# A two-layer cross-attention and FFN kernel on one core: keys and values split into high and low parts in the first stage, the routing step folded into the last stage, and three smaller reorderings

## What is computed

```python
x = x + L0_xattn(layernorm(x), ctx)     # 16 heads, scores through a latent of 32 numbers per context row
x = x + L0_ffn(layernorm(x))            # one 512x512 product, int4 weights dequantised, bias
x = x + L1_xattn(layernorm(x), ctx)     # 16 query heads of 96, 4 K/V heads; keys and values from
                                        # concat([ctx, layernorm(x)]): 1601 + 256 rows; then Wo
x = x + L1_ffn(layernorm(x))            # H + delta, below

# L1_ffn: H = x W^T + b ; z = x A (rank 32)
# logits = 0.5 * H_slice / max|H_slice| + 0.5 * delta_slice / max|delta_slice|   (maxima over ALL batches)
# probs = softmax(logits) ; soft top-2 weights w ; delta = ((z * (w @ LiMEs)) @ Bmat) * 0.5
```

## Time and profile before

| | |
|---|---|
| median of 3 runs | 2047.75 us (2040.28 to 2049.16) |
| profiled execution: time, span | 2043.46 us, 2041.7 us |
| mean granted TensorE clock | 0.950 |
| busy: PE, DVE, ACT, POOL | 94%, 55%, 46%, 32% |
| stage 1, to its last PE work | 0 to about 304 us |
| stage 2 | 309 to 1021 us |
| stage 3 | 1024 to 2006 us |
| stage 4 | 2009 to 2042 us |

### The profile page before, as it was taken

How to read it: one execution, slowest core, us unless ns; L and a number is a source line. 1 busy time by engine, 2 the same in 40 slices (tenths; PEclk the granted TensorE clock), 3 DMA queues, 4 the chain that set the end, 5 groups by cost and what they waited for, 6 DMA issues and landing times. The chain is left out here.

```text
span 2041.7 us, 23682 instructions
## 1 busy us (share of the span) xinstructions
PE 1922.5 (94%) x8690; PEld 1368.1 (67%) x8690; DVE 1118.8 (55%) x2093; ACT 944.3 (46%) x1826; POOL 653.1 (32%) x504
## 2 busy tenths in 40 slices
PE   6999998999999999998869999999999999999986
PEld 6999984444555556464637777767777777777752
DVE  1433325666666665652266666666666566664433
ACT  1332322444344334343127666655666466665640
POOL 0000000000000000000028777756776577765740
PEclk9999995999899999999769999999999999999996
DMA  5556733000111010010261232213222222212112
GB/s 176 157 170 204 226 121 70 1 11 17 50 34 42 31 42 27 11 52 26 80 167 45 75 85 75 60 30 86 74 72 75 76 79 62 56 49 57 31 31 97
DMA packets 109697, 149.51 MB, mean 73 GB/s; under 512 B 28777, under 2 KB 87529, under 8 KB 106510
## 3 DMA queue, kind: packets, MB, share of 16 engines
q1 hardware_dynamic: 101630, 145.36, 24.9%
q10 hardware_dynamic: 7952, 2.64, 0.6%
HBM read 96.52 MB, written 51.39 MB: 72 GB/s over the span
## 5 line engine op out<-in xcount | busy, mean ns | idle before, releaser
L1366 POOL TENSOR_TENSOR pl<-pf,ph 128x512 fp32r<-128x512 f32 (+1 forms) x480 | 640.9, 1352 | 300.9 <-ACT pf L1533 299.2
L1530 ACT ACTIVATE ph<-ps 128x512 fp32r<-128x512 f32 (+1 forms) x480 | 288.5, 601 | 352.8 <-PE ps L1437 351.8
L1605 DVE TENSOR_REDUCE pm<-ps 128x1 f32<-128x464 f32 (+1 forms) x512 | 317.9, 635 | 119.9 <-PE ps L1383 113.5
L1132 DVE TENSOR_REDUCE pm<-ps 128x1 f32<-128x400 f32 (+1 forms) x512 | 264.2, 567 | 103.1 <-PE ps L970 100.2
L1031 ACT ACTIVATE pr<-ps 128x512 f32<-128x512 f32 (+1 forms) x416 | 219.4, 602 | 194.3 <-PE ps L909 193.0
L1533 ACT ACTIVATE pf<-ps 128x512 f32<-128x512 f32 (+1 forms) x480 | 289.2, 603 | 0.2 <-POOL pl L1366 0.2
L1355 POOL MEMSET vf<- 128x96 f32 x1 | 0.2, 178 | 711.2 <-POOLq L685 711.2
L1383 PE MATMUL ps<-kh,qh 96*128 96x464 f32 (+1 forms) x512 | 199.6, 399 | 21.9 <-DMA ql<-q_scr 12.9
L922 PE MATMUL ps<-pr,cv 128*64 128x512 f32 (+1 forms) x832 | 208.1, 616 | 0.0
L1435 PE MATMUL ps<-qh,kh 104*128 104x512 f32 (+1 forms) x480 | 194.7, 406 | 1.4 <-issue 1.4
L1452 PE MATMUL ps<-ph,vh 128*97 128x512 f32 (+1 forms) x480 | 194.3, 405 | 0.0
(11 more groups left out here) (222 smaller groups left out, 2648.8 us busy)
## 6 DMA issues: line engine op xcount, KB each, us to landing
woT<-wo_turned SPq DMA_DIRECT2D x16, 1536.0 KB, 9.2
cnat<-in_ctx_dram SPq DMA_DIRECT2D x16, 768.0 KB
q_scr<-qst SPq DMA_DIRECT2D x48, 256.0 KB, 2.4
kf<-k_scr SPq DMA_DIRECT2D x16, 696.4 KB, 4.8
vf<-v_scr SPq DMA_DIRECT2D x16, 672.0 KB
v_scr<-vst SPq DMA_DIRECT2D x64, 144.0 KB, 2.3
k_scr<-kst SPq DMA_DIRECT2D x36, 192.0 KB, 4.7
wo_turned<-wo_out SPq DMA_DIRECT2D x32, 192.0 KB, 2.8
```

The lines of the kernel that those rows point to most:

```text
L1132: dve.reduce_max(pm[:, j, ch:ch + 1], src[:, 0:cuts[ch][1]], AX).then_inc(done["dve"], 1)
L1366: pool.tensor_tensor(pl[0:m, n % 2, cols], pf[0:m, half, :], ph[0:m, n % 2, cols].bitcast(F32), ALU.subtract).then_inc(plo, 1)
L1530: act.activation(ph[0:keys[kt], n % 2, cols], src, ACT.Exp, scale=S1).then_inc(phi, 1)
L1605: ins = dve.reduce_max(pm[:, j, ch:ch + 1], at[:, 0:cuts[ch][1]], AX)
```

## The change

Five things are changed together.

* **Split in the first stage.** Keys and values are split into high and low parts while they are in PSUM in `context_products` (ACT high, DVE low, for every group), `k_scr` and `v_scr` hold both parts, and `grouped_attention` loads them straight into `kh`, `kl`, `vh`, `vl`. `kst` has one buffer for each j and `vst` one in all. The values lie in `v_scr` by row, so that one head's load takes runs of 96 numbers (384 B).
* **First step of the third stage prepared in the second.** Three SBUF tensors `home` outlive the stages; the keys and queries of step 0 are loaded into them by `load_first_group`, and step 0's maxima run beside step 15 of stage 2 (`maxima` with `s <= S`). Units 5 to 9 of batch 2 move from steps 14 and 15 into `after()`.
* **Routing in the third stage.** `mixture` is gone: x, z and the small tiles stay in SBUF, and the H product of the last batch is issued between routing steps.
* **Norms.** `layernorm` calls back for one item at seven points rather than for two at three.
* **Small loads** are issued by SP ahead of the key stores of pieces 1 to 4. The norm of batch 0 moves from piece 2 to piece 6.

```diff
-def layernorm(dve, chain, out, x, st, mv, v, t, u, y, pause=lambda: None):
+def layernorm(dve, chain, out, x, st, mv, v, t, u, y, pause=lambda: None, between=lambda: None):
+    between()
     chain.link(dve.bn_stats(st[:, 0, :], x[:, 0, :]))
+    between()
     chain.mark(dve.bn_stats(st[:, 1, :], x[:, 1, :]))
...
     for i in range(TT):
+        between()
         last = dve.tensor_scalar(out[:, i, :], x[:, i, :], mv[:, i, 0:1], y[:, i:i + 1], ALU.subtract, ALU.mult)
```

First stage, ACT and DVE (the SP side stores both parts: keys by j as before, values in one DMA for three tiles rather than four):

```diff
+            def values_hi(n, t):
+                m = rows_in(n, t)
+                act.wait_ge(*turned(("v", n, t)))
+                if t == 0 and n:
+                    act.wait_ge(v_st, v_stored(n - 1))
+                act.copy(vst[0:m, 0, t, :], bank_of(("v", n, t))[0:m, HD0:WV]).then_inc(v_hi, 1)
...
+            def keys_lo(n, j):
+                k = SIZES[n % NP]
+                dve.wait_ge(k_hi, n * KB + j + 1)
+                dve.tensor_tensor(kst[j][:, 1, 0:k], bank_of(("k", n, j))[:, 0:k], kst[j][:, 0, 0:k], ALU.subtract)\
+                    .then_inc(done["dve"], 1)
...
-                if n == 0:
-                    load_small()
...
                 if n + 2 < N:
                     load(n + 2)
+                load_small(n)
```

Second stage:

```diff
         def maxima(s, first, end):
-            return [("max", s, i) for i in range(first, end)] if s < S else []
+            return [("max", s, i) for i in range(first, end)] if s <= S else []
...
         def after():
             e = B - 1
-            return [("raise", S - 1), ("xt", e, 0, 0), ("xt", e, 0, 1), ("ffn", e, 0), ("ffn", e, 1),
+            return [("raise", S - 1), ("q", e - 1, 5), ("q", e - 1, 6), ("xt", e, 0, 0), ("xt", e, 0, 1),
+                    ("ffn", e, 0), ("ffn", e, 1), ("q", e - 1, 7), ("q", e - 1, 8), ("q", e - 1, 9),
                     ("xt", e, 1, 0), ("xt", e, 1, 1)] + [("q", e, u) for u in range(NU)]
...
+                    act.copy(qst[:, u % 2, 0, 0:width(u)].bitcast(F32R), src[:, 0:width(u)]).then_inc(qhi, 1)
```

Third stage (`FIRST = 4`):

```diff
             if s == 0:
-                return maxima
+                return [None] * 12 + maxima
...
+            load_v(0, 0, FIRST, v0_in)
+            load_values(0)
+            load_k(1, 0)
+            load_q(1, 0)
             load_wo(0)
             load_x(0)
...
             for s in range(S):
...
+                sp.wait_ge(s_mm, (s + 1) * KT * 2)
                 if s + 3 < S:
+                    load_k(s + 3, 0)
+                    load_q(s + 3, 0)
+                if s + 2 < S:
+                    load_k(s + 2, 1)
+                    load_q(s + 2, 1)
+                    sp.wait_ge(av_mm, (s + 1) * KT)
+                    load_values(s + 2)
...
+            pe.wait_ge(to_pe, 2)
+            pe.matmul(bank(3)[:, 0:2], ones2[:, :], dg[:, :], start=True, stop=True).then_inc(from_pe, 1)
+            for t in range(TT):
+                for c in range(DC):
+                    pe.matmul(bank(t), xT[:, c, t * P:(t + 1) * P], w1T[:, c, :], start=(c == 0), stop=False)
+            pe.wait_ge(to_pe, 3)
```

More of the change, by code:

```diff
@@ L1458, in values @@
                 mm.then_inc(av_mm, 1)
-            pe.wait_ge(const, 5)
-            for item in beside(-1):
-                ring_item(*item)
-            max_rows(0)
-            pe.wait_ge(w_small, 48)
             for s in range(S):
+                if s == 1:
+                    pe.wait_ge(w_small, 48)
                 items = iter(beside(s))
@@ L1489, in _ @@
                 ring_item(*item)
+            pe.wait_ge(exp_done, 2 * S * KT)
+            pe.wait_ge(o_done, 2 * S)
+            pe.wait_ge(mix_ones, 2)
+            pe.wait_ge(to_pe, 1)
+            pe.matmul(bank(2)[0:2, 0:P], pmx[:, :], ident[:, :], start=True, stop=True).then_inc(from_pe, 1)
+            pe.wait_ge(to_pe, 2)
[4 more added lines that the diff above has]
+            pe.wait_ge(to_pe, 3)
+            for b in range(B):
+                mm = pe.matmul(bank(2)[0:NE, b * P:(b + 1) * P], wt[:, b, :], ident[:, :], start=True, stop=True)
+            mm.then_inc(from_pe, 1)
+            pe.wait_ge(to_pe, 4)
+            pe.wait_ge(w_mix, 48)
+            pe.matmul(bank(3)[0:R, :], li[:, :], wT[:, :], start=True, stop=True).then_inc(from_pe, 1)
+            pe.wait_ge(bm_done, 1)
+            for n in range(B * TT):
+                b, t = divmod(n, TT)
+                if t == 0:
+                    pe.wait_ge(zp_done, b + 1)
+                if 4 <= n < (B - 1) * TT:
+                    pe.wait_ge(y_done, n - 3)
+                pe.matmul(delta_bank(n), zp[:, b, t * P:(t + 1) * P], bm[:, :], start=(b < B - 1), stop=True)\
+                    .then_inc(d_mm, 1)
         @block.scalar
@@ L1762, in _ @@
             link = chain.link
             flat = "p b e -> p (b e)"
-            for i, s in enumerate((h8all, dlall)):
-                sf = s[:, :, :].rearrange(flat)
+            dve.wait_ge(ring_done, len(ring))
+            for i, rows in enumerate((h8all, dlall)):
+                sf = rows[:, :, :].rearrange(flat)
                 link(dve.scalar_tensor_tensor(ab[:, i, :], sf, -1.0, sf, ALU.mult, ALU.max))
```

703 lines of the change are left out of this document (288 added, 415 removed).

## The result

| | before | after |
|---|---|---|
| median | 2046.57 us, 4 runs (2040.28 to 2049.16) | 1998.74 us, 4 runs (1992.77 to 2000.29) |
| profiled execution: time, span | 2043.46, 2041.7 us | 1992.77, 1991.0 us |
| mean granted clock | 0.950 | 0.965 |
| busy: PE, DVE, ACT, POOL | 94%, 55%, 46%, 32% | 96%, 54%, 46%, 31% |

The account below looks back on a forecast made before the run. PE, busy 9 tenths nearly everywhere, was taken as the bound, so only less work, fewer gaps or less half clock helps. Terms summed to -57.8 us on 2043.5, giving 1985.7; the forecast was 1987 us, range 1970 to 2006.

Parts of the forecast that it names:

- Hand-over, -31: Stage 2 to stage 3: scores follow the barrier at once, 5.2 us remain of 37.1; -31 us (-27 to -34).
- The rival of a clock that stays at half: Hand-over and final deltas: half clock lasts longer, 7 us more and 3 more, giving 1997 us; chance 0.08.
- Routing, -10.5: Kernel's end, from the last xT: H runs beside the routing, 37.5 us instead of 48.0; -10.5 us (-5 to -18).
- End of stage 2, -5: Steps 14, 15 and `after()`: moved units fill PE gaps, unit 9's copy waits for a store; -5 us (-1 to -9).
- Small loads, -9.3: Stage 1: issuing on SP spares PE 6.13 us of wait and 3.2 of half clock; -9.3 us (-6 to -10).
- Splitting in stage 1, +4: Stage 1: +1 us behind the last tile, +3 for DMA engines just full; +4 us (0 to +15).
- the slower rival: Stage 1: one `vst` buffer makes value copies wait for the previous piece's store, eating the gain of 58 us; chance 0.02.
- My sign of being wrong: Stage 1: the prediction is wrong if PE waits for DMA there; one of three such signs, no size given.
- the share over 0.9: Stage 1: the new profile would show a DMA share over 0.9 from 170 to 262 us.
- Norms of stage 2, -9: Three norms of stage 2: single reads split the stall into 0.3 to 1.2 us gaps, clock full; -9 us (0 to -13).
- the rival "norms do nothing": Norms of stages 2 and 3: seven reads do nothing or harm, 2006 us, either alone 1997; chance 0.10 together.
- Norms of stage 3, +3: Three norms of stage 3: tenth maximum comes 4.1 us late rather than 3.2; +3 us (-3 to +13).

Follow-up runs that it names:

- qst3: Changed kernel with a staging buffer of its own for unit 9 of the ten projection units; ratio 0.9794 to the kernel before.
- n2_old: Changed kernel with stage 2's norms back to two ring reads at three points, stage 3 keeping the new ones; ratio 0.9800 to the kernel before.
- h_first: Changed kernel with the last batch's 16 H matmuls ahead of the two small routing matmuls rather than behind them; ratio 0.9805 to the kernel before.
- small_only: Kernel before with only the small loads moved to SP, and with them batch 0's norm and the dequantising moved; ratio 0.9949 to the kernel before.
- w_early: Changed kernel with the first wo group earlier and the third later in pieces 8 to 12, same bytes; ratio 0.9721 to the kernel before.
- half_v: Changed kernel storing only the high part of the context values, which stage 3 reads twice; ratio 0.9761 to the kernel before.
- control: The changed kernel unedited, measured again; ratio 0.9790 to the kernel before.
- spread: Changed kernel with the last 15 wo groups two in each of pieces 8 to 15, not three in 8 to 12; ratio 0.9733 to the kernel before.

## Why the prediction was right, and where its sizes were off

**Hand-over, -31.** Right. 4.41 us from the last matmul to the first scores (5.2 forecast; its own parts, 3.6 and 1.4, give 5.0). The rival of a clock that stays at half is out: it rose after at most 10.2 us in every profile. The first step is 51.3 us long, where it was 48.3: 9.5 us of its work are at half clock, where 5.3 were, and PE idles 0.6 us, most of it for the queries of step 1. In qst3 and n2_old the scores are at half clock for 3.4 us only, and the step is no shorter (50.6 and 50.9 us), since the maxima then wait 1.4 and 1.6 us for those queries: the slow scores cover a load.

**Routing, -10.5.** Right, measured -11.0. H covers the chain of small instructions, and h_first shows what the cover is worth: 8 us.

**End of stage 2, -5.** Measured -8.3. The wait of unit 9 on the store of unit 7 came as described, 3.90 us; 2.25 of it go with a buffer of its own. The term was too small mostly in its clock: work at half clock in this stretch fell from 15.1 to 3.8 us, which at full clock takes 5.7 us less, and I had 3, for the FFN product. PE's idle time fell by 9.7 us, where the forecast's parts give 8.4 (11.2 of units put into gaps, 2.8 of new gap). That split is read from the two profiles; no run undid this part alone.

**Small loads, -9.3.** Right, measured -9.2 in small_only.

**Splitting in stage 1, +4: mis-sized.** Against small_only (297.0) the changed stage 1 (305.9 to 311.8) is 9 to 15 us longer; without the first two stretches, which scatter in themselves, 9 to 13. I had the DMA engines as the price and `vst`'s one buffer as the slower rival's place. What holds PE is the wait one step ahead of it, at the third wo group, whose buffer the first one's store must free; it was in the trace of before, 3.43 us of it, and I had not listed it, since no gap on PE stood behind it. My sign of being wrong, PE waiting for DMA in stage 1, so came true by way of ACT and DVE. Without that wait w_early is at 300.5, 3.5 above small_only. Some 1.5 of these are in the first two stretches; from there to the last transposes of context both take 220.2 us, and the stretch behind them takes 38.1 us instead of 36.1. In half_v, with half the value bytes stored, it takes 36.1 again, so the 2.0 us go with the low part of the values. So splitting by itself costs 2, all at the end, where I had 1, and nothing by full engines, where I had 3. The Trainium skill, "DMA: Bandwidth & Descriptors", Specifications, gives some 358 GB/s as HBM's limit for a core; over stretches of 26 us and more the rows here stay under it, with the engines at 1.00 of their time at 305, while single slices of 1.2 us reach 419 (control, 186 to 234 us). The demand of 302 that I worked out is borne out by the 297 that w_early and 287 that spread move from 170 to 262, at 0.92 and 0.90; the changed kernel, which stalls there, moves 272 at 0.86, not the share over 0.9 that I foretold.

**Norms of stage 2, -9: wrong in its clock.** I let the clock stay at full behind gaps of 0.3 to 1.2 us, arguing from one gap in stage 3. In the norm shown the gaps are smaller than sized (1.7 us for 3.3), but the half clock came too, in the changed kernel's profile 6.8 us behind each of the three, and 3.4 at a fourth norm. For stage 2 this is the rival "norms do nothing", which had a chance of 0.10 together with its half in stage 3. Over all profiles the new reads are worth 1 us.

**Norms of stage 3, +3: near in size, not in kind.** Measured +5.1 between the two profiles and +5.7 on average over the ten with the new reads. I had DVE falling further behind, 4.1 us rather than 3.2 at each norm. But PE's idle time is what it was, 2.44 us for 2.36, only in fewer pieces (2.01 us the largest, 2.4 foretold); the steps are longer because the clock falls to half behind the norm, and without that they take 69.9 us for 69.4. So 1.5 of the 5 us are there in every run, and the rest is luck of the clock.

These errors do not all cancel: stage 1 (with splitting) and the norms of stage 2 gave some 13 us less than the sum had, the norms of stage 3 some 2 less and the hand-over 1 less, the end of stage 2 some 3 more and the routing 0.5 more, which leads from 1987 to the 1999 measured. That is the upper end of the forecast's own range of 1975 to 1999, which is too narrow upwards: the terms' bounds as independent (the root of the sum of their squares) give 12 us down, but 19 up, to 2006. The sum was right in kind because 51 of its 58 us (loads, hand-over, routing) hung on waits seen in the trace of before, with work beside them that could be named.
